# Windowed attention in three chained blocks: in the first attention, the second-half values of the preceding chunk are issued ahead of the first round's transposes of probabilities

## What is computed

```
h = layer_norm(x); q, k, v = split(h @ w_qkv.T)            # 16 heads of width 16
kcat, vcat = keys and values of the chunk before and of this chunk (128 + 128)
scores = q @ kcat^T * scale, valid where i + 1 <= j <= i + 128
attn = softmax(scores); out = attn @ vcat
x = x + out @ w_o.T
```

## Time and profile before

| what | value |
|---|---|
| median of 3 runs | 1790.45 us (1790.11 to 1791.4) |
| span of the profiled execution | 1791.1 us (its time as a run is not listed apart; the three runs lie within 1.3 us of each other) |
| PE busy | 1731.2 us, 97% of the span |
| PEld busy | 1496.0 us, 84% |
| DVE busy | 1494.1 us, 83% |
| ACT busy | 1197.5 us, 67% |
| POOL busy | 1080.0 us, 60% |
| mean granted TensorE clock | 0.994 |
| first attention | from about 18 us to about 375 us of the span |

### The profile page before, as it was taken

How to read it: one execution, slowest core, us unless ns; L and a number is a source line. 1 busy time by engine, 2 the same in 40 slices (tenths; PEclk the granted TensorE clock), 3 DMA queues, 4 the chain that set the end, 5 groups by cost and what they waited for, 6 DMA issues and landing times.

```text
span 1791.1 us, 43798 instructions
## 1 busy us (share of the span) xinstructions
PE 1731.2 (97%) x15424; PEld 1496.0 (84%) x15424; DVE 1494.1 (83%) x3797; ACT 1197.5 (67%) x3088; POOL 1080.0 (60%) x1060
## 2 busy tenths in 40 slices
PE   6999999999999999999999999989999999999997
PEld 4778777789998888888887888878888888888886
DVE  6888988868878898888987678789898898967776
ACT  6999988854445787877876334358787877743332
POOL 3676556534434778778773455377878777634343
PEclk9999999999999999999999999999999999999999
DMA  3111211032322111111112434331111111131221
GB/s 107 38 37 38 67 44 31 26 107 75 108 63 99 48 41 54 44 52 51 44 43 71 147 105 126 100 103 41 52 44 55 41 54 47 31 102 56 82 82 36
DMA packets 139812, 116.03 MB, mean 65 GB/s; under 512 B 10584, under 2 KB 138848, under 8 KB 138848
## 3 DMA queue, kind: packets, MB, share of 16 engines
q1 hardware_dynamic: 139616, 113.53, 20.5%
HBM read 75.74 MB, written 37.75 MB: 63 GB/s over the span
## 4 chain that ended last, share of the span: by engine, by line
PE 84%; DVE 9%; ACT 3%; issue 3%; POOL 0%; DMA 0%; SPq 0%; DVEq 0%; POOLq 0%; ACTq 0%
PE psum L567 17%; PE psum L569 17%; PE psum L568 17%; PE psum L906 6%; PE psum L874 5%; PE psum L887 5%; PE psum L682 3%; PE psum L664 3%; PE psum L848 3%; ACT a_probs L1718 2%; PE psum L920 2%; PE psum L617 1%; DVE a_neg_max L1211 1%; DVE psum L1209 1%; PE psum L654 1%
## 5 line engine op out<-in xcount | busy, mean ns | idle before, releaser
L1837 ACT ACTIVATE b_probs<-masked,neg_max 128x256 f32<-128x256 f32 (+1 forms) x512 | 250.6, 494 | 124.3 <-DVE neg_max L1343 124.3
L1343 DVE CUSTOM_DVE_ANT_0 masked<-psum,mask 128x256 f32<-128x256 f32 (+1 forms) x512 | 177.3, 412 | 75.9 <-PE psum L874 75.9
L567 PE MATMUL psum<-wa_hi,b_h_hi 128*128 128x512 f32 (+1 forms) x576 | 233.8, 406 | 6.9 <-DVE wa_lo L1138 3.9
L568 PE MATMUL psum<-wa_lo,b_h_hi 128*128 128x512 f32 (+1 forms) x576 | 214.0, 372 | 0.0
L569 PE MATMUL psum<-wa_hi,b_h_lo 128*128 128x512 f32 (+1 forms) x576 | 214.0, 372 | 0.0
L567 PE MATMUL psum<-g_h_hi,wm_hi 128*128 128x512 f32 (+1 forms) x480 | 190.5, 397 | 2.7 <-POOL g_h_lo L2121 1.6
L2070 POOL TENSOR_TENSOR g_in<-g_in,minus_half 128x16 f32<-128x16 f32 x64 | 188.2, 2940 | 4.5 <-DVE g_in L1295 4.5
L568 PE MATMUL psum<-g_h_lo,wm_hi 128*128 128x512 f32 (+1 forms) x480 | 189.3, 394 | 0.0
L569 PE MATMUL psum<-g_h_hi,wm_lo 128*128 128x512 f32 (+1 forms) x480 | 189.2, 394 | 0.0
L1458 POOL TENSOR_TENSOR g_in<-g_z,g_in 128x512 f32<-128x512 f32 x62 | 79.8, 1287 | 143.4 <-DVE g_in L1289 138.2
L567 PE MATMUL psum<-wm_hi,u_hi 128*128 128x256 f32 x576 | 164.3, 285 | 0.1
(11 more groups left out here) (169 smaller groups left out, 5644.0 us busy)
## 6 DMA issues: line engine op xcount, KB each, us to landing
x_mid<-y_out SPq DMA_DIRECT2D x96, 128.0 KB, 1.7
rope_in<-in_rope SPq DMA_DIRECT2D x64, 128.0 KB, 2.2
x_res<-x_state SPq DMA_DIRECT2D x64, 128.0 KB, 2.2
g_in<-x_mid SPq DMA_DIRECT2D x32, 256.0 KB, 3.8
g_old<-x_state SPq DMA_DIRECT2D x16, 512.0 KB, 4.0
out_x<-g_fin SPq DMA_DIRECT2D x15, 512.0 KB, 2.9
w_raw<-in_w_mlp_b SPq DMA_DIRECT2D x2, 2154.0 KB, 8.8
x_in<-in_x SPq DMA_DIRECT2D x32, 128.0 KB, 2.2
```

The lines of the kernel that those rows point to most:

```text
L567: nc.tensor.matmul(out, a_hi, b_hi, start=first, stop=False)
L568: nc.tensor.matmul(out, a_hi, b_lo, start=False, stop=False)
L1343: ins = nc.vector.tensor_tensor_reduce(out[:, at], src[:, at], (mask if now else mask0)[:, at], -1.0, BIG, ALU.add, ALU.min, neg_max[:, r, ...
L1837: ins = nc.scalar.activation(out, src, ACT.Exp, bias=neg_max[:, r, k:k + 1], scale=-1.0, accum_out=row_sum[:, n % 2, 4 * r + k:4 * r + k + 1])
```

## The change

`values(s - 1, 1)` and `transpose_probs(4s)` change places in TensorE's list. No instruction is added, removed or altered, and the lists of the other engines stay as they are.

```diff
                     transpose_z(s + 2)
                 if a_chunk(s + 1) and s > -1:
                     project_qk(s + 1)
-                if a_chunk(s):
-                    transpose_probs(4 * s)
                 if a_chunk(s - 1):
                     values(s - 1, 1)
                 if a_chunk(s):
+                    transpose_probs(4 * s)
                     scores(s, 1)
                     transpose_probs(4 * s + 1)
```

## The result

The changed kernel has a median of 1794.65 us over 20 runs (1792.38 to 1795.82), the kernel before one of 1791.45 us over 20 runs (1788.98 to 1793.43). The ratio is 1.0018 with a 95% interval of 1.0011 to 1.0024: 3.2 us slower, or 2.0 to 4.3 us. The direction was forecast, the time lies in the range, and the size is little more than half of the 5.8 us of the sum. It is just inside the 0.2% that the prediction called no change. The forecast of 1796.2 us stood on a median of 1790.45 from three runs; over 20 runs it is 1.0 us higher, so the time is nearer to the forecast (1.6 us) than the difference is (2.6 us).

A forecast was written before the change was run, and what follows sets the result against it. PE was taken to bound the stage, with ACT close behind. 28 steps at 0.20 us (5.6) plus 0.2 for step 31 gave +5.8 us on 1790.45, so 1796.2 us, range 1791.8 to 1799.0.

The forecast's parts named there:

- the 5.8 us of the sum: 28 steps at 0.20 us make 5.6, plus 0.2 for step 31: 1796.2 us against the median of 1790.45.
- the 0.2% that the prediction called no change: Whole kernel: 0.2% (3.6 us) is about what a measurement can tell from no change; chance of staying within it 0.26.
- The values would wait for POOL instead of ACT: PE behind project_qk, step 12: values start 0.12 us behind POOL's select(47), at 152.47, 0.64 earlier than before.
- The rival that put POOL's result at 0.03: POOL's result reaches PE after 0.03 us instead of 0.12: 0.11 a step, 3.1 us, 1793.5; chance 0.22.
- The transposes 1.02 us behind the values' start: PE, step 12: values' loads take 0.82 us, then 0.20 idle; transposes start at 153.49, 0.96 later than before.
- The scores would not be touched: PE, step 12: scores start at 154.08 by PE's list, 154.06 at the earliest by ACT, not 154.12: 0.04 us gained.
- The copy would wait: ACT, step 12: copy_probs(48) waits for the moved transposes, starting at 154.18, 0.35 us later; 0.20 is left on the path.
- `q_twice` "takes 0.67": ACT, step 12: q_twice starts 0.47 us after copy_probs, takes 0.67, ends at 155.32; project_v then starts at 155.38.
- Rival 2: ACT before project_v: the copy's delay is absorbed, only the scores' gain counts; 1.7 us less, 1788.8; chance 0.06.
- The next transposes "lie inside": PE, step 12: transposes of round 49 start at 154.90 against 154.79, reaching 155.29, before project_v at 155.38.
- 28 steps, and step 17 free: Steps 2 to 30 without 17 cost 0.20 us each, 5.6 in all; steps 1 and 17 cost nothing.
- Step 31 (+0.2): Step 31, with other work in between: 0.2 us more, as in the others (nothing to 0.4).

The follow-up runs named there:

- doubled select: POOL's p_before select in the last round of each chunk done twice, on both kernels: ratio to the kernel before 1.0015 in the old order, 1.0135 in the changed one.
- split wait: Changed kernel with the values' wait split, so matmuls reading p_before wait only for the first select: 0.9985, 1788.94 us against 1792.05 for the kernel before.
- before_q_first: Kernel before, with q_twice ahead of copy_probs(4s) in ACT's list: 1.0046, 1799.70 us against 1792.05.
- after_q_first: Changed kernel, with q_twice ahead of copy_probs(4s) in ACT's list: 1.0058, 1800.93 us against 1790.06 for the kernel before.
- around_by_round: Changed kernel with the values in two halves by round, one before and one behind the transposes: 1.0104, 1809.15 us against 1790.06 for the kernel before.
- after_select_twice: Changed kernel with POOL's p_before select in the last round of each chunk done twice: 1.0135, 1815.48 us against 1792.05 for the kernel before.

## Why the prediction was right in its mechanism and high in its size

- **The values would wait for POOL instead of ACT.** Right to the hundredth: 0.12 us from select to load. The doubled select showed it by intervention. The rival that put POOL's result at 0.03 gave the difference nearest to the measured one (+3.1 against +3.2 us), by the wrong term: that is luck.
- **The transposes 1.02 us behind the values' start.** 1.04: the loads took 0.85 instead of 0.82, and the gap behind them was 0.20 as taken.
- **The scores would not be touched.** They start 4.32 us behind the step's first transposes (155.38 - 151.06) where it was 4.36 (154.12 - 149.76): a gain of 0.04, as forecast. The three changes of shape did not add up on PE's path. Behind the values' start the gaps are 0.20 and 0.17, as large together as the two before; the third, 0.36 where nothing hides it (split wait), lies inside the wait for POOL. The rule that a change of mode drains the TensorE, which the prediction cites from the Trainium skill's page "TensorEngine Tiling (Array Packing)", section Tiling Modes (Key Properties), agrees with these gaps; the cost of the change does not come from it.
- **The copy would wait.** 0.03 behind the transposes, as taken; shown as the only way in which the change costs by the pair with `q_twice` first.
- **The term that was too large: `q_twice` "takes 0.67".** It takes 0.59 here. The 0.67 was read from a row in which it stood in ACT's list right behind a copy that had not waited; in the changed kernel the copy in front of it has just come out of a wait. The copies show the same pair of values: 0.60 after a wait, 0.66 without. The ends lose nothing by it: `q_twice` ends 0.48 behind the copy's end in both kernels (154.49 and 154.97, 156.09 and 156.57). So part of the recorded time of an activation that has not waited is not work on the path. The start came 0.49 behind the copy's instead of 0.47, and the select ended 2.57 us into the step instead of 2.59. Together: 0.20 + 0.02 (values) + 0.02 (start) - 0.08 (`q_twice`) - 0.02 (select) = 0.14; `project_v` moved by 0.15, and the step length says 0.13. Rival 2 had named this place: copy and `q_twice` closer together after an idle ACT. It asked for 0.20 and got 0.06 (1.14 us from the start of the one to the end of the other before, 1.08 now).
- **The next transposes "lie inside".** They do, by 0.04 only. They start 0.11 behind the copy's end (156.09 to 156.20), not 0.06. With the 0.39 that they take up to `project_v` before, as in the run `before_q_first` (158.49 to 158.88), they would release PE at 156.59; `q_twice` does so at 156.57 + 0.06 = 156.63, where `project_v` starts. `before_q_first` shows that the transposes alone would hold it too. The idle that the prediction expected in front of `project_v` doesn't show, as PE is still recorded as loading until 156.62; it stands as 0.28 in front of these transposes.
- **28 steps, and step 17 free.** The length of step 17 grew by 0.08 us, from 10.71 to 10.79, not by nothing; its copy and `q_twice` were not late, and why it grew stays open. The distance between the loads of step 29 and step 30 shrank, from 11.54 to 11.28 us, so that the changed profile is behind by 3.42 us at the first of these and by 3.16 at the second. That too is without an explanation here, and it is why 3.6 us of steps are 3.3 us at step 31.
- **Step 31 (+0.2).** It had another sign. At the start of step 31 the changed profile is behind by 358.09 - 354.80 = 3.29 us, at the first matmul of the next stage (L567 on `g_h_hi`, 368.85 against 366.36) by only 2.49. The last section has what is known of that.

## What to carry to other kernels

A stall says that its engine has time there, not that anything can use it: before moving work into it, look up when that work's own inputs come, here 0.12 us before the stall's end, and who waits for the work that is pushed back. In a list that runs in order a result that was early by 0.65 us can become late, and the waits of the edited engine don't say so: it showed on the neighbour, as an idle in front of a copy that names the transposes, and on PE only as idle under "issue", which names no one. And when a wait is the price of a new order, ask whether all of the waiting work needs it: splitting it turned +0.18% into -0.15% (the interval is 0.06% to 0.24%).

## What the hardware showed beyond that

**Time goes by the matmuls of one column tile.** The trace lists two records for each of these matmuls. Weights of 128 x 32 on two of the four column tiles took 0.81 us for 16 records, and on all four 0.82 us for 32: eight records to a tile either way. With 16 records on all four tiles, four to a tile, the loads took 0.38 us. Leaving tiles empty saves nothing; giving each tile less does.

**The gap at a change of shape isn't one number.** From `project_qk`, whose matmuls have 512 columns, to the values the loads idle 0.36 us where nothing else holds them (the runs with the split wait and with the values by round). From the transposes, of 128 columns, to the same values it is 0.17, from the values to the transposes 0.20. No run tells what the length depends on.

**The recorded duration of a short activation depends on what was in front of it.** `q_twice` has 0.66 to 0.67 us behind work without a wait, 0.59 behind a copy that had waited; `copy_probs` has 0.66 and 0.60. A path that is summed from durations of instructions that stood in line comes out long; their ends give the right distance (0.48 us here in both cases).

**TensorE's clock at the stage's end.** The windows of the kernel before, from step 31 on (the eighth column is the share of full clock that was granted):

```profile
361.40:364.00 2.60, 0.71 (x8) 0.54 (x12) 2.57 (x4) 2.31 (x9) 2.13 (x3) 1.00 0.00 0
364.00:368.00 4.00, 4.00 (x41) 3.34 (x39) 1.22 (x2) 2.29 (x6) 2.15 (x4) 0.57 0.00 0
```

and of the changed one:

```profile
364.70:367.20 2.50, 0.70 (x9) 0.46 (x10) 2.46 (x4) 2.50 (x11) 2.02 (x4) 1.00 0.00 0
367.20:370.40 3.20, 2.98 (x44) 2.47 (x44) 0.46 (x2) 2.37 (x6) 3.06 (x5) 1.00 0.00 0
```

After two idle stretches of PE in step 31, of 1.24 and 1.90 us, the kernel before runs at the lower level, 1.2 GHz, for most of 4 us (0.57 on the mean). The changed kernel idles 1.20 and 1.80 us there and keeps 2.4 GHz. That fits the 0.8 us that it gets back of its 3.3. The profiles of all four kernels with the old order of these two blocks have such a stretch at this place (mean clock from 350 to 385 us: 0.95). Of the six with a new order three have it too: `after_q_first` and `around_by_round` with 0.95, and `after_select_twice`, which gets there 20 us later, with 0.66 from 386 to 391 us. It is one execution each, and profiles lose clock at other places too (the changed kernel has 0.96 in its first 40 us, the kernel before 1.00). Whether the order keeps the clock up there, or chance does, stays open; no run was made for it. The profile of the split wait keeps its clock there, so some 0.9 us of its 3.1 us may not be the steps': 28 x 0.08 = 2.2 us are. The interval of that ratio, 1.1 to 4.3 us, holds both.
